# The second layer of an MLP as three products of high and low parts, in a four-layer graph network kernel

## Time and profile before

| | |
|---|---|
| median of three runs | 3992.46 us |
| the profiled execution | 3984.56 us, its span 3982.8 us |
| TensorE matmul busy | 3709.5 us, 93% |
| VectorE busy | 3101.9 us, 78% |
| ScalarE busy | 1994.8 us, 50% |
| GpSimd busy | 1576.2 us, 40% |
| chain that ended last | TensorE 78%, VectorE 10%, ScalarE 4% |

### The profile page before, as it was taken

How to read it: one execution, slowest core, us unless ns; L and a number is a source line. 1 busy time by engine, 2 the same in 40 slices (tenths; PEclk the granted TensorE clock), 3 DMA queues, 4 the chain that set the end, 5 groups by cost and what they waited for, 6 DMA issues and landing times.

```text
span 3982.8 us, 59433 instructions
## 1 busy us (share of the span) xinstructions
PE 3709.5 (93%) x19042; PEld 2707.6 (68%) x19042; DVE 3101.9 (78%) x5637; ACT 1994.8 (50%) x3047; POOL 1576.2 (40%) x980
## 2 busy tenths in 40 slices
PE   7999579999999999999999999999999999999986
PEld 6888346676667766666666676766677666666665
DVE  6787557888887888888888888888878888888752
ACT  4656145555555555555545545555555555555430
POOL 4667234333443444444433333334434444444310
PEclk9999689999999999999999999999999999999986
DMA  8988322222222212222222222222222212222200
GB/s 286 317 310 298 93 53 64 70 69 69 63 58 69 60 52 56 53 69 69 69 69 69 69 69 69 69 69 63 58 69 59 58 52 53 69 69 69 53 16 11
DMA packets 195935, 341.10 MB, mean 86 GB/s; under 512 B 28720, under 2 KB 64432, under 8 KB 195888
## 3 DMA queue, kind: packets, MB, share of 16 engines
q1 hardware_dynamic: 195888, 340.50, 30.3%
HBM read 188.89 MB, written 50.33 MB: 60 GB/s over the span
## 4 chain that ended last, share of the span: by engine, by line
PE 78%; DVE 10%; ACT 4%; issue 3%; POOL 2%; DMA 2%; SPq 1%; DVEq 0%; ACTq 0%; POOLq 0%
PE bank L1444 12%; PE bank L1495 12%; PE obank L1378 12%; PE bank L1233 9%; PE pair L1233 7%; PE pair L1362 7%; PE bank L1406 6%; PE bank L1463 3%; PE pair L1339 3%; DVE minus_max L1033 2%; PE obank L1265 2%; DMA pT<-in_adjT 2%; PE bank L1265 1%; DVE b_st L841 1%; ACT hsq L632 1%
## 5 line engine op out<-in xcount | busy, mean ns | idle before, releaser
L602 POOL TENSOR_TENSOR pT<-pT,node_edge 128x1024 f32<-128x1024 f32 x256 | 628.6, 2462 | 532.0 <-ACT pT L690 530.1
L690 ACT ACTIVATE pT<-pair 128x1024 f32<-128x1024 f32 x512 | 515.9, 1031 | 325.6 <-PE obank L1378 248.2
L1033 DVE TENSOR_REDUCE minus_max<-pair 128x2 f32<-128x1024 f32 x512 | 603.3, 1216 | 56.9 <-PE pair L1339 56.5
L1023 DVE TENSOR_TENSOR pT<-pT,node_edge 128x1024 f32<-128x1024 f32 x256 | 399.8, 1562 | 269.4 <-ACT pT L690 266.2
L1495 PEld LDWEIGHTS bank<-v,p3T 128*128 128x128 f32 x4096 | 502.4, 199 | 36.2 <-DVE p3T L1182 24.5
L1495 PE MATMUL bank<-v,p3T 128*128 128x65 f32 x4096 | 499.8, 280 | 20.2 <-DVE p3T L1182 20.2
L540 POOL TENSOR_TENSOR d_rs<-d_ve,minus_half 128x4 f32<-128x4 f32 x32 | 32.2, 1007 | 1207.5 <-DVE d_ve L853 1207.5
L1378 PE MATMUL obank<-pT,v 128*64 128x512 f32 x2048 | 490.3, 611 | 8.4 <-POOL pT L602 4.8
L1444 PE MATMUL bank<-w_s,hid 128*128 128x256 f32 x2048 | 479.6, 389 | 0.3 <-DVE hid L1112 0.3
L1444 PEld LDWEIGHTS bank<-w_s,hid 128*128 128x128 f32 x2048 | 383.6, 192 | 87.7 <-issue 40.1
L632 ACT ACTIVATE p3T<-x,d_sh,d_rs 128x256 f32<-128x256 f32 x128 | 66.4, 589 | 720.6 <-POOL d_sh L546 720.6
(11 more groups left out here) (189 smaller groups left out, 6468.7 us busy)
## 6 DMA issues: line engine op xcount, KB each, us to landing
pT<-in_adjT SPq DMA_DIRECT2D x64, 512.0 KB, 5.3
a_at<-in_adjT SPq DMA_DIRECT2D x64, 512.0 KB, 3.6
q_parts<-high_parts SPq DMA_DIRECT2D x256, 128.0 KB, 4.7
k_parts<-high_parts SPq DMA_DIRECT2D x256, 128.0 KB, 4.1
b_at<-in_adjT SPq DMA_DIRECT2D x64, 512.0 KB, 3.9
hid<-in_x SPq DMA_DIRECT2D x32, 512.0 KB, 4.4
x_res<-hid SPq DMA_DIRECT2D x32, 512.0 KB, 5.0
pre_bn<-hsq SPq DMA_DIRECT2D x32, 512.0 KB, 4.1
```

Of the source, the lines that this page charges most:

```text
L602: nc.gpsimd.tensor_tensor(half, half, node_edge[:, 0:2, :], ALU.mult).then_inc(a_masked[0].sem, 1)
L690: nc.scalar.activation(dst, pair[p][:, :, :], func, **more).then_inc(a_copied[p].sem, 1)
L1023: nc.vector.tensor_tensor(half, half, node_edge[:, 2:4, :], ALU.mult).then_inc(a_masked[1].sem, 1)
L1033: nc.vector.tensor_reduce(minus_max[:, t, 2 * two_heads:2 * two_heads + 2], pair[p][:, :, :], AX.X, ALU.max, negate=True).then_inc(a_copie ...
```

## The change

`W2` (times half the rms weight) is kept as a high and a low part, made once at the start from raw weights that lie in buffers not yet in use. For each graph the gated activations `hsq` are split likewise: new tokens `b.gate` (ScalarE) write `hid_high` over `hid`, new tokens `b.rest` (VectorE) write `hid_low` over the ring `hsq`. `b.out2` has eight tokens instead of four, one for each 128 hidden channels, each with all four node blocks and three float32r products; a tanh that reuses a ring slot waits for the `b.out2` that read it. The high parts of queries and keys lie in `pT`, `a.nat` reads them from `q_parts` and `k_parts`, so that a new token `p.sorth` (8 of the 24 sorting transfers) comes before it. The eight rows of `a.putshift` go in one transfer. `ORDER` is another one.

```
 ORDER = """
-a.exp00:2 a.max11:1 a.max20:1 a.scores11:1 b.hid3:2 b.hidc1:3 a.exp01:2 a.max21:1 b.rrms:3 b.hidc2:3 a.scores20:1
-a.scores21:1 a.mask6:2 b.eye:2 a.max30:1 h.spread0:3 b.hid4:2 a.max31:1 b.x30:3 a.values00:1 a.values01:1 a.scores30:1
-b.x31:3 h.values00:3 a.exp10:2 a.exp11:2 b.stats3:3 a.mask7:2 h.values01:3 a.scores31:1 a.exp20:2 b.hidc3:3 a.exp21:2
-b.hid5:2 h.spread1:3 a.scores40:1 a.scores41:1 b.hid6:2 b.hidc4:3 b.rstd3:3 a.xmid0:2 p.sortk:1 a.exp30:2 b.hid7:2
-a.exp31:2 a.values10:1 a.values11:1 a.scores50:1 b.hidc5:3 a.max40:1 h.values10:3 a.max41:1 h.values11:3 a.headc0:2
-a.xmid1:2 a.max50:1 a.max51:1 a.scores51:1 b.sum:2 a.scores60:1 h.spread2:3 b.rstd:2 b.hidc6:3 a.values20:1 b.bias:2
-a.bias:1 b.hidc7:3 b.stats:2 a.mask0:1 a.mask1:1 a.exp40:2 a.max60:1 a.load:0 a.scores61:1 a.values21:1 a.scores70:1
-a.exp41:2 a.exp50:2 a.max61:1 h.values20:3 b.factors:3 b.spread:2 a.headc1:2 a.scores71:1 b.sumsq1:2 p.flip:0
-h.values21:3 a.max70:1 a.exp51:2 a.exp60:2 p.norm:1 a.max71:1 a.values30:1 h.spread3:3 a.values31:1 b.sumsq2:2
-a.exp61:2 b.low:3 b.vcol:3 b.aggl0:2 a.putshift:1 a.mask2:1 a.exp70:2 p.q0:0 b.aggl1:2 b.v3c0:3 a.edges1:1 p.q1:0
-p.k0:0 p.k1:0 p.x1:0 b.sumsq3:2 b.v3c1:3 a.vmask0:1 h.values30:3 a.headc2:2 p.v0:0 a.exp71:2 p.flipc:1 a.mask3:1
-b.sumsq4:2 b.tanh0:3 p.v1:0 h.values31:3 b.tanh1:3 a.load0:0 a.nat00:0 a.nat01:0 b.out20:2 a.nat10:0 a.headc3:2
-a.vmask1:1 p.qhigh:1 a.nat11:0 b.tanh2:3 b.out21:2 h.prob0:3 a.vmask2:1 h.head0:3 a.nat20:0 a.nat21:0 b.out22:2
-a.nat30:0 a.nat31:0 a.vmask3:1 b.out23:2 a.wo0:1 a.nat40:0 b.tanh3:3 a.nat41:0 p.khigh:1 h.prob1:3 a.wo1:1 a.vmask4:1
-a.nat50:0 h.head1:3 p.vc:1 b.norm3:3 b.ms:2 a.vmask5:1 a.nat51:0 b.flip30:2 b.sumsq5:2 a.nat60:0 h.prob2:3 b.sumsq6:2
-b.flip31:2 a.div0:1 b.diag:2 a.nat61:0 b.e:2 a.vmask6:1 a.nat70:0 b.sumsq7:2 b.scale0:2 b.scale1:2 a.vmask7:1
-h.head2:3 a.nat71:0 p.flipl:0 b.scale2:2 b.flip3c0:3 h.prob3:3 b.agg0:1 b.flip3c1:3 a.mask4:1 a.shift:0 b.silu0:2
-b.silu1:2 b.scale3:2 b.vt:2 b.agg1:1 b.norm:2 b.v30:2 p.qlow:0 b.hid0:1 b.hid1:1 a.scores00:0 b.load:1 h.store:3
-b.silu2:2 b.silu3:2 b.exps:3 p.klow:0 a.scores01:0 b.hid2:1 b.aggc0:2 a.div1:1 a.mask5:1 a.load1:0 b.v31:2
-a.scores10:0 a.shiftc:1 p.rstd:0 a.max00:0 a.max01:0 b.edges:2 b.aggc1:2 a.max10:0 b.hidc0:2 p.sortq:0 a.edges0:0
-h.head3:3
+p.qhigh:3 p.sortq:1 b.out24:5 a.nat10:3 a.max20:3 b.out25:5 b.x30:5 a.headc3:4 a.nat11:3 b.out26:5 b.load:2 a.load1:1
+h.store:4 p.sortk:1 a.nat20:3 p.khigh:3 b.gate1:5 a.load:0 b.tanh2:5 a.max21:3 b.out27:5 b.x31:5 p.vc:3 a.nat21:3
+b.tanh3:5 a.wo0:4 a.nat30:3 a.nat31:3 a.xmid0:4 a.wo1:4 b.gate2:5 b.stats3:5 a.nat40:3 b.gate3:5 b.norm3:5 a.nat41:3
+b.flip30:5 b.flip3c0:5 a.max30:3 a.mask1:3 b.flip31:5 a.nat50:3 a.nat51:3 a.max31:3 b.e:5 b.flip3c1:5 a.nat60:3
+b.sumsq1:4 p.rstd:2 a.nat61:3 b.agg0:4 a.xmid1:4 a.max40:3 b.norm:4 b.exps:5 b.vt:5 a.max41:3 b.sumsq2:4 a.mask2:3
+a.nat70:3 b.stats:4 a.nat71:3 b.agg1:4 a.shift:3 b.v30:5 b.aggc0:4 b.hid0:4 a.scores00:3 b.aggc1:4 a.mask3:3 a.max50:3
+b.v31:5 a.scores01:3 a.shiftc:3 b.sumsq3:4 a.scores10:3 b.hidc0:4 a.exp00:3 a.exp01:3 a.exp10:3 b.hid1:4 a.max51:3
+b.eye:4 b.factors:5 a.max60:3 a.max61:3 b.hid2:4 a.max70:3 b.vcol:5 b.aggl0:4 a.max71:3 b.hidc1:4 b.aggl1:4 a.exp11:3
+b.sumsq4:4 a.scores11:3 b.hidc2:4 a.edges1:3 b.hid3:4 a.scores20:3 b.sumsq5:4 a.scores21:3 a.values00:3 a.exp20:3
+b.hidc3:4 b.v3c0:5 p.x1:2 a.vmask0:3 a.vmask1:3 a.exp21:3 b.low:5 b.v3c1:5 h.prob0:5 a.values01:3 a.vmask2:3
+h.spread0:5 b.hidc4:4 h.head0:5 a.vmask3:3 a.putshift:1 b.sumsq6:4 h.prob1:5 b.hid4:4 b.hid5:4 a.vmask4:3 a.exp30:3
+a.scores30:3 h.head1:5 a.mask4:3 a.scores31:3 h.values00:5 b.hidc5:4 a.exp31:3 b.sumsq7:4 h.values01:5 b.hid6:4
+a.headc0:3 a.scores40:3 b.ms:4 a.vmask5:3 h.spread1:5 a.mask5:3 a.scores41:3 a.div0:3 p.norm:2 b.diag:4 b.hidc6:4
+a.values10:3 a.exp40:3 a.values11:3 h.prob2:5 b.hid7:4 a.scores50:3 a.exp41:3 h.values10:5 a.scores51:3 h.values11:5
+b.hidc7:4 b.sum:4 a.scores60:3 a.scores61:3 b.scale0:4 h.spread2:5 a.values20:3 a.exp50:3 a.values21:3 b.rrms:4
+b.scale1:4 a.vmask6:3 p.flipl:2 a.scores70:3 a.mask6:3 b.spread:4 a.vmask7:3 a.exp51:3 b.silu0:4 a.scores71:3 p.flip:2
+a.headc1:3 b.scale2:4 h.values20:5 b.scale3:4 a.exp60:3 a.values30:3 b.rest0:4 b.silu1:4 a.mask7:3 p.qlow:2 a.exp61:3
+h.head2:5 p.q0:2 a.values31:3 a.load0:0 p.q1:2 a.div1:3 p.klow:2 h.values21:5 a.exp70:3 p.k0:2 b.rest1:4 a.edges0:2
+h.prob3:5 a.headc2:3 b.rstd3:4 p.flipc:2 a.exp71:3 p.k1:2 b.silu2:4 b.edges:4 b.out20:4 p.v0:2 h.spread3:5 p.v1:2
+b.tanh0:4 b.silu3:4 b.rest2:4 a.max00:2 b.tanh1:4 b.gate0:4 a.max01:2 h.head3:5 b.rest3:4 b.out21:4 b.out22:4
+a.max10:2 p.sorth:0 b.rstd:3 b.bias:3 a.bias:2 a.max11:2 b.out23:4 h.values30:5 h.values31:5 a.nat00:2 a.mask0:2
+a.nat01:2
 """.split()
...
-        w2_s = sb("w2_s", P, KH, D)
+        w2_s = sb("w2_s", P, 2, KH, D, dt=f32r)
...
-        q_high, k_high = (high_parts[:, i] for i in range(2))
+        q_high, k_high = (pT[:, 0, i * K:(i + 1) * K] for i in range(2))
...
+            def place(dst, i, c, src, done):
+                r = DH1
+                sp.dma_start(dst[c * r:(c + 1) * r, i::P // r, :].bitcast(f32), src[i * r:(i + 1) * r]).then_inc(done.sem, 16)
+            def sort_high(g):
+                for u, dst, src in ((U_Q, q_parts, q_high), (U_K, k_parts, k_high)):
                     p, n = a_unit(u)
                     sp.wait_ge(*a_copied[p].upto(g, n + 1))
+                    for i in range(P // DH1):
+                        place(dst, i, i % 2, src, a_hh_in)
...
             def put_shift(g):
                 sp.wait_ge(*o_copied.upto(g, 1))
-                for h in range(H1):
-                    sp.dma_start(q_parts[ROW_SHIFT:ROW_SHIFT + 1, h, :].bitcast(f32),
-                                 shiftT[h:h + 1, :].bitcast(f32)).then_inc(a_shift_in.sem, 16)
+                sp.dma_start(q_parts[ROW_SHIFT:ROW_SHIFT + 1, :, :].bitcast(f32),
+                             shiftT[:, :].bitcast(f32)).then_inc(a_shift_in.sem, 16)
...
+            act.wait_ge(setup.sem, 1)
+            for t in range(KH):
+                src = raw2[2 * t // KH][:, t % (KH // 2), :]
+                nc.scalar.activation(w2_s[:, 0, t, :], src, ACT.Copy, scale=half_rms[:, t:t + 1]).then_inc(w2_high.sem, 1)
...
             def b_tanhs(n):
                 def f(g):
                     for t in (2 * n, 2 * n + 1):
-                        act.wait_ge(*b_norm.upto(g, t + 1))
+                        p, c = b_unit(V_RB)
+                        act.wait_ge(*(b_norm.upto(g, t + 1) if t < KH - 1 else b_copied[p].upto(g, c + 1)))
                         if t >= RING:
-                            act.wait_ge(*b_gated.upto(g, t - RING + 1))
+                            act.wait_ge(*b_out_used.upto(g, t - RING + 1))
...
+            def b_gate(n):
+                def f(g):
+                    for t in (2 * n, 2 * n + 1):
+                        act.wait_ge(*b_gated.upto(g, t + 1))
+                        nc.scalar.activation(hid_high[:, t, :], hsq[:, t % RING, :], ACT.Copy).then_inc(b_high.sem, 1)
...
+            def b_rest(n):
+                def f(g):
+                    for t in (2 * n, 2 * n + 1):
+                        dve.wait_ge(*b_high.upto(g, t + 1))
+                        nc.vector.tensor_tensor(hid_low[:, t % RING, :], hsq[:, t % RING, :], hid_high[:, t, :].bitcast(f32),
+                                                ALU.subtract).then_inc(b_low.sem, 1)
...
-            def b_out2(t):
+            def b_out2(k):
                 def f(g):
+                    pe.wait_ge(*b_low.upto(g, k + 1))
+                    for t in range(T):
+                        if k == 0 and t % 2 == 0:
+                            b_free(g, V_OUT + t // 2)
+                        p, _ = b_unit(V_OUT + t // 2)
+                        dst = bank[p][:, (t % 2) * D:(t % 2 + 1) * D]
+                        rows = slice(t * P, (t + 1) * P)
+                        for n, (x, y) in enumerate(PRODUCTS):
+                            i = nc.tensor.matmul(dst, hid_low[:, k % RING, rows] if x else hid_high[:, k, rows], w2_s[:, y, k, :],
+                                                 start=k == 0 and t % 2 == 0 and n == 0,
+                                                 stop=k == KH - 1 and t % 2 == 1 and n == len(PRODUCTS) - 1)
+                        if k == KH - 1 and t % 2 == 1:
+                            i.then_inc(b_filled[p].sem, 1)
+                    if k < KH - 1:
+                        i.then_inc(b_out_used.sem, 1)
```

More of the change, by code:

```diff
@@ L237, in gnn_stack @@
         setup = signal("setup", 10)
+        w2_high = signal("w2_high", KH)
+        w2_low = signal("w2_low", KH)
         c_x_in = [signal(f"c_x_in{i}", 1, 16) for i in range(2)]
@@ L821, in _ @@
                 **{f"b.aggc{j}": b_agg(j) for j in range(K)},
-                **{f"b.hidc{t}": b_hid(t) for t in range(KH)}, **{f"b.tanh{n}": b_tanhs(n) for n in range(4)},
```

(17 more changed lines are left out.)

87 lines of the change are left out of this document (52 added, 35 removed).

## The result

The changed kernel takes 4057.79 us (4043.56 to 4060.12), the kernel before in the same comparison 3990.99 us (3987.18 to 3992.93): a ratio of 1.0161, 95% interval 1.0136 to 1.0186. It is slower by 1.6%; I had forecast 3950 us and a range up to 4045.

The account below looks back on a forecast made before the run. TensorE was taken to bound leg A (44.8 us) and VectorE leg B (59.7): a step of 104.5 us against 105.8. 30 x -1.3 and -4 at the ends gave -43 from 3992.5, say 3950 us, range 3892 to 4045.

Parts of the forecast that it names:

- The product: `b.out2` on TensorE: 96 float32r matmuls a graph at 0.119 us, 11.4 us, saving 3.2 us a graph.
- The rests: Eight added `b.rest` operations a graph on VectorE, in leg B: 0.60 us each, 4.8 us.
- the gates: Eight added `b.gate` copies a graph on ScalarE: 0.65 us each, 5.2 us, costing only as a link in a chain.
- the covers that I had called thin: Margins keeping VectorE from waiting in leg B: 0.65 us before `rest2`, 1.2 before `silu2`; chance they are gone 0.13.
- Leg A: From `a.shift` to the next first `b.scale`: TensorE stays its bound, 49.45 us falls to 44.8.
- Leg B: From the first `b.scale` to `a.shift`: VectorE bounds it, 58.5 + 0.65 + 0.5 = 59.7 us, against 56.4 before.
- rival 2: TensorE's clock falls in leg B, over `b.agg0` and `b.agg1`: step 108.0 us, 4055 us in all; chance 0.25.
- Rival 1: TensorE stays the bound, the rests cost nothing: step 102.7 us, 3895 us in all; chance 0.17.
- Rival 4: Rests meet GpSimd's operations, each losing up to 0.87 us: +7 us a step, 4160 us in all; chance 0.03.
- The signs: Wrong if `b.rest` takes much over 0.6 us, VectorE waits over 1 us a step for `b.gate`, or leg B's clock falls below 0.95.
- Ends: First graph and last two graphs of the pass: together -4 us.
- row transfer: The shift's rows in one transfer instead of eight, in leg A: the gain is used up, worth nothing.

Follow-up runs that it names:

- e2: The changed kernel with VectorE's `b.diag` moved ahead of `a.div0` in the order, same work: 4149.32 us, ratio 1.0388 against the kernel before.
- e1: The changed kernel with the four `b.diag` operations on ScalarE instead of VectorE: 3982.44 us, ratio 0.9972 against the kernel before.
- e3: The changed kernel with the eight `b.rest` operations a graph on GpSimd instead of VectorE: 4044.52 us, ratio 1.0121 against the kernel before.
- e8: e1 with the rests on GpSimd as well: 3979.54 us, ratio 0.9961 against the kernel before.
- e13: e11 with `a.nat00` and `a.nat01` ahead of `h.values31` on TensorE: 3967.99 us, ratio 0.9935 against the kernel before.
- e10: e1 with fourteen needless transposes of a constant in three gaps of TensorE: 3970.87 us, ratio 0.9939 against the kernel before.
- e6: The kernel before with the shift's eight rows in one transfer, nothing else changed: 3994.09 us, ratio 1.0003.
- e11: e10 with the rests on GpSimd as well: 3963.43 us, ratio 0.9920 against the kernel before.
- e5: The kernel before with eight more VectorE subtractions of 128x512 a graph, one behind each silu: 4109.10 us, ratio 1.0288.

## Why the prediction was wrong, step by step

- *The product, 11.4 us a graph.* Right: the 96 matmuls run at the pace of `p.v`, in groups of twelve in 1.41 us at full clock (I had 1.43).
- *The rests, 0.60 us each, the gates 0.65.* Right in size (in the changed kernel's trace two rests take VectorE 1.2 us; gates 149.5 / 256 = 0.58). The rests never waited for their gates (idle 0.0 in their group); the covers that I had called thin held.
- *Leg A, the first step that failed.* Following "At its end VectorE does `h.head1`, `ms`, `vmask5`, `div0`, `diag`", I gave the diagonal its length of before, 0.87 us, and nothing for GpSimd's mask beside it. It took 2.78, and leg A ended at 46.91 instead of 44.8. The collision is 2.78 - 0.87 = 1.91 of these 2.1 us: e2 has the diagonal at 0.87 away from the mask, and in e1, without it on VectorE, the leg is 44.21. Against the forecast leg A is 30 x 2.1 = 63 of the 108 us by which it missed; e1's edit itself is worth 75 us (4057.79 to 3982.44).
- The mechanism stood in the prediction. I had weighed it on a mask and followed only the eight rests through the new order, not every VectorE operation whose neighbours on GpSimd the order changed. The Trainium skill, "SBUF — State Buffer", "Who interferes with whom", names `tensor_scalar` among the operations that can take the port pair shared with GpSimd, if their operands allow it. The trace agrees (0.87 and 2.78 us for the same four instructions), and the small one of `p.x1` went from 0.23 to 1.75 us on average, ending with GpSimd's masks too. Some instructions behind it TensorE waits 0.6 us for `v` in leg A, in the changed kernel and in e1 alike; no run takes that apart.
- *Leg B, the second that failed: 58.5 us of VectorE, plus 0.65 and 0.5.* The work was right (36.79 + 21.47 = 58.3 us busy), the bound was not. In the head TensorE is the bound at 97% (e3, e8, e13); VectorE's waits are 0.9 us there and 2.3 in the tail, 3.2 in all where I had 1.15. I had TensorE idle for 7 us in leg B; in the step shown it is busy for 56.16 of 60.69 us. A sum over one engine can't hold for a leg whose bound changes inside it. The 1.7 us of the miss come to 30 x 1.7 = 52 us.
- *The rest of the 108 us.* 63 and 52 and 1 at the ends are 116. The other 8 went the other way: I added 7.9 us for the distance of the median from the profiled execution, and in the changed kernel the median lies 0.7 below it.
- *The clock, rival 2 at 4055 us.* The time was nearly this one, its mechanism mostly not: `b.agg1` never ran at the low level. The level began earlier, 4.9 to 8.2 us into the tail and so around `b.flip31`, and reached into `b.agg0` in 9 of 25 steps, with tails of 24.70 to 25.72 us; the others are 22.93 to 23.60. My reason against it, that stretches with gaps of 1.5 us mostly kept the clock, was a wrong reading: in the trace of before such a gap (1.48 us) starts each tail, and 19 of 25 tails have a stretch at the low level, their mean granted clock 0.86. An estimate of its share: e10's tails with both aggregations at full clock are 22.65 us, the changed kernel's mean is 23.78, so some 1.1 of leg B's 1.7 us is the low level, and 37.65 + 22.65 = 60.3 is left, 0.6 over my 59.7. The fills gave back 0.3 to 0.5 of it. The rests' price in leg B is 0.6 us or less (e3; 0.05 between e1 and e8). What holds the last 0.6 us, and what an order with both an early `b.norm` and undelayed maxima would give, stays open.
- *Rival 1, TensorE the bound everywhere, 3895.* Refuted by the tail, where it is busy for 84%, part of that at the low level. *Rival 4, rests beside GpSimd.* They never met, but its mechanism decided the case on another operation.
- *The signs.* Of those that I had named for being wrong one came: the clock row of leg B is 0.94. VectorE was busy for 3357 us, not 3256; the groups `diag` and `a_ve` grew by 57.1 + 48.6 = 106 us, which covers it. In leg B VectorE is busy for 96% and TensorE for 93%, where I had said over 97 and under 90.
- *Ends, -4, row transfer 0.* Right: about -3, and e6.

The best version found is e11: 0.8% faster than before and, by the quotient of the two ratios (0.9920 / 1.0161), 2.4% faster than the change as given.

## What to carry to other kernels

When an order of work changes, list every VectorE operation that now lies beside a GpSimd elementwise one, old operations too, and price each as ending with its neighbour; put a small one that gates TensorE on ScalarE. Where a stretch has steps at both clock levels, compare steps of the same level before reading a mean. Before summing an engine's work over a stretch, find where inside it the last wait changes hands, and sum each part for its own engine. Less work for a matmul engine that waits for another one can make the kernel slower.

## What the runs showed of the hardware

- Four 128x128 `TENSOR_SCALAR` of 0.87 us ended with GpSimd's 128x1024 `TENSOR_TENSOR`, at 2.78 us, though they had started 0.56 us before it.
- Removing 7.6 us of matmuls a step brought a wait of 2.5 us and 20 us at 1.2 GHz behind it: ratio 1.0469 against 1.0161 with them.
- Behind one wait of 2.03 us, 24 matmuls took 4.63 us instead of 3.04 (e5); behind one of 1.76 us, 16 took 2.98 instead of 2.00 (e2).
- In the tail of the changed kernel TensorE waited 1.21, 0.72, 0.71 and 0.69 us with matmuls between, and `b.flip31` behind these took 1.11 us where `b.flip30` took 0.65.
